# One 67-row load per expert split into loads of 64 and 3 rows in a vision and mixture-of-experts kernel

## What is computed

```
h = tok(x)                                  # three levels, joined, @ Wf.T + bf
h = h + attn(layernorm(h))                  # 12 heads, elu(q)+1, elu(k)+1
h = h + ffn(layernorm(h))                   # rmsnorm, gate, top 4 of 16 experts
# one expert: hid = t @ mlp1_w.T + mlp1_b ; a = swiglu(hid) ; y = a @ mlp2_w.T + mlp2_b
# E = 16 experts, width 192, hidden 384 (mlp1 gives 768 columns)
```

## Time and profile before

| | us |
|---|---|
| median of 3 executions | 805.46 |
| lowest, highest | 795.44, 820.06 |
| profiled execution, first to last instruction | 824.0 |
| PE busy in it | 531.0 |
| DVE busy in it | 335.4 |
| ACT busy in it | 245.6 |
| POOL busy in it | 317.4 |

### The profile page before, as it was taken

The page is one execution under the profiler, slowest core; times in us unless marked ns, Lnnn a source line. Parts: engine busy times, 40 slices in busy tenths (PEclk is TensorE's granted clock), DMA queues, the critical chain, the costliest instruction groups (busy, mean ns, idle before and its releaser), DMA issues.

```text
span 824.0 us, 12035 instructions
## 1 busy us (share of the span) xinstructions
PE 531.0 (64%) x2852; PEld 339.4 (41%) x2853; DVE 335.4 (41%) x881; ACT 245.6 (30%) x637; POOL 317.4 (39%) x458
## 2 busy tenths in 40 slices
PE   0000522266999999996499577777777777777750
PEld 0000400052445555565355355555545555455440
DVE  0222344433222332333875254455444444444430
ACT  0232222221212122211100244444444444444430
POOL 7770000000011101113000366766776666667671
PEclk9999999996555555555555699999999999999995
DMA  6332222243000000000001123332323333333334
GB/s 188 92 102 88 88 88 89 71 99 103 1 0 10 10 10 10 10 10 11 16 29 39 41 43 50 54 49 46 54 45 50 50 50 48 50 52 50 45 55 86
DMA packets 36575, 42.82 MB, mean 52 GB/s; under 512 B 8424, under 2 KB 27898, under 8 KB 36554
## 3 DMA queue, kind: packets, MB, share of 16 engines
q0 software_dynamic: 17456, 19.79, 15.1%
q1 hardware_dynamic: 17388, 21.98, 8.7%
q10 hardware_dynamic: 1710, 0.80, 0.4%
HBM read 27.97 MB, written 14.59 MB: 52 GB/s over the span
## 4 chain that ended last, share of the span: by engine, by line
PE 37%; SPq 17%; issue 14%; POOL 13%; ACT 7%; DVE 4%; POOLq 4%; DMA 4%; ACTq 0%; DVEq 0%
SPq L232 13%; POOL acc_odd L365 4%; PE bank L948 3%; POOL R L350 3%; PE bank L947 3%; POOL out L365 3%; POOLq L370 3%; SPq L231 3%; DMA R<-in_m 2%; PE bank L1100 2%; POOL ixr L371 2%; PE bank L1070 2%; PE bank L1082 2%; ACT R L845 2%; ACT R L836 2%
## 5 line engine op out<-in xcount | busy, mean ns | idle before, releaser
L350 POOL DMA_INDIRECT R<-t_dram,ixr x86 | 88.6, 1030 | 68.9 <-POOL ixr L371 59.4
L695 DVE TENSOR_SCALAR R<-bank 128x384 f32<-128x384 f32 x82 | 45.7, 558 | 166.1 <-PE bank L1104 166.1
L1100 PE MATMUL bank<-W1s,R 128*128 x164 | 54.5, 332 | 76.5 <-ACT R L837 55.5
L841 ACT ACTIVATE R<-bank 128x384 f32<-128x384 f32 x82 | 40.3, 491 | 167.7 <-PE bank L1104 167.7
L365 POOL DMA_INDIRECT out<-R,ixr x40 | 64.5, 1611 | 30.1 <-ACT R L863 16.8
L1116 PE MATMUL bank<-W2s,R 128*128 x720 | 73.2, 246 | 3.4 <-issue 3.4
L365 POOL DMA_INDIRECT acc_odd<-R,ixr x40 | 66.1, 1653 | 12.7 <-issue 12.7
L316 POOL TENSOR_SCALAR R<-R 128x2 f32<-128x2 f32 x8 | 3.0, 377 | 156.4 <-DVE R L556 156.4
L371 POOL COPY ixr<-Li 128x1 int32 x80 | 61.0, 762 | 0.0
L1116 PEld LDWEIGHTS bank<-W2s,R 128*128 128x128 f16 x720 | 55.7, 97 | 8.6 <-issue 5.0
L1100 PEld LDWEIGHTS bank<-W1s,R 128*128 128x128 f16 x164 | 16.1, 98 | 99.4 <-issue 94.2
(11 more groups left out here) (216 smaller groups left out, 1107.3 us busy)
## 6 DMA issues: line engine op xcount, KB each, us to landing
R<-in_m SPq DMA_DIRECT2D x16, 288.0 KB
h_all<-in_m1a SPq DMA_DIRECT2D x11, 384.0 KB
h_all<-in_m1c SPq DMA_DIRECT2D x11, 201.0 KB
WA<-in_m1a SPq DMA_DIRECT2D x5, 384.0 KB
acc_odd<-lz SPq DMA_DIRECT2D x17, 96.0 KB, 1.9
W1s<-W1s SPq DMA_DIRECT2D x1, 1536.0 KB, 10.1
t_dram<-R SPq DMA_DIRECT2D x8, 192.0 KB, 2.0
out<-h_all SPq DMA_DIRECT2D x8, 192.0 KB, 2.0
```

Source lines behind the costliest of these rows:

```text
L350: po.indirect_dma_start(out=Gr32[:, slot, :], out_offset=None, in_=t_dram, in_offset=bass.IndirectOffsetOnAxis(ap=ixr[:, slot:slot + 1], a ...
L695: ve.tensor_scalar(lin[:, p, :], bank[2 + 2 * p][:, 0:HID], (LIMIT + 1) * S1, (1 - LIMIT) * S1, ALU.min, ALU.max).then_inc(s_lin, 1)
L1100: mm(o, Ct[:, p, 0, :], W1s[:, e, 0, c], start=True, stop=False)
```

## The change

The load of the 67 rows (L231) becomes two: rows 0 to 63 (D1 is 64) and rows 64 to 66. Both go to the same places as before. Since each transfer adds 16 to the buffer's semaphore, ScalarE waits for 64 an expert where it waited for 48.

```diff
             def load_expert(e, k):
                 sp.dma_start(stA[k], m1a[e, :, :].rearrange("e p n -> (e p) n")).then_inc(s_st[k], 16)
-                sp.dma_start(stC[k], m1c[e, :, :].rearrange("e p n -> (e p) n")).then_inc(s_st[k], 16)
+                sp.dma_start(stC[k][0:D1, :], m1c[e, 0:D1, :].rearrange("e p n -> (e p) n")).then_inc(s_st[k], 16)
+                sp.dma_start(stC[k][D1:67, :], m1c[e, D1:67, :].rearrange("e p n -> (e p) n")).then_inc(s_st[k], 16)
                 sp.dma_start(stD[k], m2[e, :, :].rearrange("e p n -> (e p) n")).then_inc(s_st[k], 16)
...
-                    ac.wait_ge(s_st[k], i * 48 + 48)
+                    ac.wait_ge(s_st[k], i * 64 + 64)
...
-                ac.wait_ge(s_st[e % STAGES], 48 * (e // STAGES + 1))
+                ac.wait_ge(s_st[e % STAGES], 64 * (e // STAGES + 1))
```

## The result

The changed kernel takes 740.35 us in the median of 4 executions (728.88, 730.53, 750.16, 756.96), the kernel before 805.98 (a fourth execution, of 806.49, has come to the three). The profiled execution is the one of 728.88 us; its span is 727.1. A second job with the same kernel gave 731.91 us (724.18 to 738.11), ratio 0.9074 (0.8971 to 0.9177); its profile is the "second profile" of this text.

The account below looks back on a forecast made before the run. The loads of 16 experts bound the loading stage, through one DMA engine. Expert 6 at 39.5 plus VectorE's 50.9 ends it at 90.4 us, not 173.9; 805.5 - 83.5 = 722 us, range 703 to 745.

Parts of the forecast that it names:

- One engine: In the expert loads, the 67-row transfer lies on one DMA engine: 8.04 + 1.68 = 9.72 us per expert, 9.79 measured.
- rival B: No change, 805 us: 25 GB/s is the pace of SyncE's descriptors, so 64 rows stay slow; chance 0.03.
- The first expert: At the start of the loading stage, the first expert is there at 11.5 us (10.4 to 13.3), before at 20.1.
- A buffer's round and expert 6: Three load buffers come round in 12.1 us, 4.0 us per expert; expert 6 begins on VectorE at 39.5 us.
- VectorE's list: From expert 6 to the stage's end, low parts and tokenizer copies: 41.05 + 5.9 + 3.9 = 50.9 us, ending at 90.4.
- Rival A: Loads spread, but the three buffers' round becomes the bound at 18.1 us; gain 65, time 741 us; chance 0.08.
- ScalarE's waits for loads over the whole stage: Sign in the loading stage: ScalarE's waits for expert loads fall from 126.6 us to about 45.
- The added transfer: SyncE's extra issue for the three rows costs one step of 1.04 us, making three issues' span 2.7 us.
- Rival C: Slower: each added issue in SyncE's queue comes on top, 16 x 0.86 = 14 us, 819 us; chance 0.03.
- The tail: From the loading stage's end at 173.9 us to the end of the span: 650 us, left as it is.
- rival D: The shifted start changes TensorE's clock in attention stage or expert loop: 680 us, or 760 or more; chance 0.06.
- The 18.5 us of the profile before: Profiled execution's excess over the median, unplaced; if the first stage had 4 us of it, the gain would be 79 to 80.

## Why the prediction was right, and where it wasn't

The forecast was 722 us with a range of 703 to 745; the measured 740.35 lies in it, near its upper end. The gain was 65.6 us where 83.5 had been forecast.

*One engine.* Right, and shown from both sides: 61 rows bring the floor and 163.6 us, 60 rows take both away, so rival B is out. The prediction had only "under a tenth" for the busy share of the 16 engines in the floor. A window inside it, 92 to 96 us of the kernel before, shows 0.06 at 25 GB/s, one sixteenth (columns as in the earlier trace rows):

```profile
92.00:96.00 4.00, 1.10 (x6) 0.64 (x4) 3.55 (x6) 0.42 (x1) 0.00 (x0) 1.00 0.06 25
```

By the Trainium skill's rule (DMA: Bandwidth & Descriptors, "Why a DMA increments its semaphore by 16 and not by 1") 60, 64 and 80 rows have large divisors up to 16, and 61 and 67 have none but 1; all five agree with the stage ends here. The other rule of the Trainium skill, that splitting by partitions isn't worth it (same page, "Rules for kernel authors"), doesn't hold for these 67 rows: split, they end the stage 83 us earlier.

*The first expert.* Taken at 11.5 us, from 10.4 to 13.3. ScalarE's wait ends at 12.6 us in the first profile and at 12.8 in the second, 1.1 to 1.3 us late and inside the bounds.

*A buffer's round and expert 6.* Taken at 39.5 us on VectorE; 40.81 in the second profile, which is the first expert's delay and no more. The two rounds took 24.0 us where two of 12.1 were forecast, but two of their terms were off and cancelled, which is luck: the four issues of an expert took 1.7 us from the first to the last (19.66 to 21.40) and not 2.7, and ScalarE began 3.6 us after the last issue (21.40 to 25.00) and not 3.0. In the first profile expert 6 began at 50.9, for SyncE's slow stretch.

*VectorE's list.* Taken at 50.9 us; from expert 6 to the end of the last L462 it is 50.0 in the second profile (40.81 to 90.76) and 49.9 in the first. The two new waits for TensorE, taken at 2.8 + 1.1 us, measure 3.2 in all. The stage ends at 90.8 against the forecast 90.4. Rival A, that the loads' round binds to the end, is out: ScalarE still waits 0.2 to 4.1 us for each load behind expert 6, 3 us or more for four of the nine, but VectorE waits for none of them. ScalarE's waits for loads over the whole stage, forecast at 45 us, are 40.6 in the second profile and 47.8 in the first:

```profile
ACT L737 <- DMA R<-in_m: 25.6, 5, 12.6
ACT W1s L737 <- DMA R<-in_m: 22.2, 9, 4.2
```

*The added transfer.* Costed at one step, 1.04 us, per round; the run with none shows no cost, and the one with three shows 0.8 us at most for two more transfers over two rounds. Rival C is out.

*The tail.* "Left as it is" is the step that was mis-sized, for a single execution: the part behind the stage took 650 us in the profile before and 626 in the one after (646 in the second profile), and 23 of these 24 us are in the attention layer, with the clock. By the prediction's own sign ("no longer 650 us") this would speak for rival D; the run with the start held back is why it doesn't. Had the attention layer's clock stayed at 0.50, as in four of the experiments' profiles (188.3 us each, like the kernel before), the first profile would have been near 750, where two of its four executions are.

*The missing 18 us.* Two things stood between 722 and 740. One is SyncE's slow stretch, 10 us in the profiled one of those four executions. Of the other three there is no trace, so it isn't shown for them, but their times speak for it. At 264 us at the low level, one of them took 730.53 us and one of the second job 724.18; at 297 and 301 us the other two took 750.16 and 756.96, where four executions of the 80-row and unrolled kernels took 741.4 to 743.9 at 301 to 306. The other thing is how the few executions fell on the clock. Compared at equal time at the low level (258 to 267 us), nine executions of the kernel before take 806 to 811 us and three of the changed one 724.2, 728.1 and 730.5: about 81 us less, against the stage's 83. The median of all eight executions of the changed kernel is 733 us, of the 30 of the kernel before 807, which is 74 us. So the gain in the stage was right to 1 us in the second profile (83.5 forecast, 83.2 measured) and 10 us too high in the first (73.1), and the number for the median was off by that stretch and by the scatter behind the stage. The range had about 10 us for the scatter and nothing for the stretch, so that 740.35 lies inside it is in part luck. Rival D, that the change itself shifts the clock, isn't shown: with the start held back the scatter stays what it was. A loss of up to some 10 us by it can't be excluded with so few executions.

*The 18.5 us of the profile before.* The prediction could not place them. They go with the clock: this profile has 0.50 throughout the attention layer and the 79 us behind it and a mean of 0.818, and the eight of the 30 executions with a mean clock of 0.814 to 0.822 took 823.8 to 827.4 us. So the clock alone accounts for them, and the loading stage needs no share.

## What to carry to other kernels

When a stage that only loads runs far below the rate that its engines reach elsewhere, look at the rate in slices shorter than one transfer: a constant floor near 25 GB/s between bursts was one transfer on one engine. The bytes on that engine, which are the whole transfer and a sixteenth of the two others, gave the period to 1% when divided by that rate. A row count such as 67 or 61 costs that; 60, 64 or a padded 80 don't, and one extra small transfer cost nothing that showed. Before forecasting the gain, write down the next list in line (here VectorE's 50 us), and judge by the end of the stage, since the median of a few executions scattered by more than two per cent for the clock alone.

## What was not expected

In one execution SyncE's instructions between 20 and 43.5 us came 0.7 us apart or in multiples of it, register moves as much as transfers. Seven other profiles with the same loop and spread loads don't show it. Its cause stays open.

GpSimd's gathers became slower beside the denser loads: 1040 ns on average in the kernel before, 1319 in the second profile of the changed kernel, and 1022 again with 61 and 6 rows, where the floor is back. Before and second profile:

```profile
L281 POOL DMA_INDIRECT R<-in_x,idx_sb x42 | 43.7, 1040 | 13.4 <-issue 12.5 <-POOL R L276 0.9
L282 POOL DMA_INDIRECT R<-in_x,idx_sb x42 | 55.4, 1319 | 13.5 <-issue 12.5 <-DMA idx_sb<-in_idx 1.0
```

The last one starts at 70.49 us, where it was 59.11, and the copy that needs it comes at 80.3. With 3.0 us to landing, as the last ones in this profile have, or 4.6, the median of all 42, some 5 to 7 us are left of the 11 that the forecast had to spare. They are left because the copy stands 10 us before the end of the stage and not 16, as the forecast had it: at the forecast's 74 us the pixels would only just have landed.
